# The attention stage of a graph network on one core: SyncE issues all transfers of a group at one moment, behind the transposes of the node rows

## The reference, cut to what matters

```python
h = (x @ gat_W).reshape(n, H, C1)
a_src = jnp.einsum('nhc,hc->nh', h, att_src)
a_dst = jnp.einsum('nhc,hc->nh', h, att_dst)
logits = jax.nn.leaky_relu(a_src[src] + a_dst[dst], negative_slope=0.2)
alpha = _segment_softmax(logits, dst, n)
msg = h[src] * alpha[:, :, None]
x1 = jax.ops.segment_sum(msg, dst, num_segments=n).reshape(n, H * C1) + gat_bias
x1 = _prelu(x1, prelu1_a)
q = x1 @ Wq + bq
k = x1 @ Wk + bk
v = x1 @ Wv + bv
```

## Time and profile before

| what | us |
|---|---|
| median of 3 runs | 6158.78 |
| lowest and highest | 6152.38, 6185.52 |
| the profiled execution, its own time | 6170.1 |
| its span, first to last instruction | 6168.3 |
| busy PE, DVE, ACT, POOL | 3904.2, 2719.5, 718.2, 3232.2 |

### The profile page before, as it was taken

The page is one execution under the profiler, slowest core; times in us unless marked ns, Lnnn a source line. Parts: engine busy times, 40 slices in busy tenths (PEclk is TensorE's granted clock), DMA queues, the critical chain, the costliest instruction groups (busy, mean ns, idle before and its releaser), DMA issues. The chain is left out here.

```text
span 6168.3 us, 73822 instructions
## 1 busy us (share of the span) xinstructions
PE 3904.2 (63%) x14562; PEld 2847.0 (46%) x14563; DVE 2719.5 (44%) x9904; ACT 718.2 (12%) x2361; POOL 3232.2 (52%) x3351
## 2 busy tenths in 40 slices
PE   3555555563556655554667666767674777777777
PEld 2343434342444444443455555555552555555555
DVE  5443434342333233332444444444453555555555
ACT  3000000000000000000111111101110212222122
POOL 5466666644555555554444444444433555555553
PEclk8677777776777777776777776777786888888889
DMA  7344444433333333332333333333322444343432
GB/s 182 80 107 106 107 105 107 106 86 88 106 107 106 106 107 107 107 101 87 89 94 97 93 97 93 96 95 95 96 78 84 113 119 122 111 119 112 118 115 84
DMA packets 334355, 636.43 MB, mean 103 GB/s; under 512 B 86166, under 2 KB 213124, under 8 KB 333828
## 3 DMA queue, kind: packets, MB, share of 16 engines
q0 software_dynamic: 159744, 441.43, 27.5%
q1 hardware_dynamic: 170437, 185.56, 9.6%
q10 hardware_dynamic: 3648, 3.67, 0.2%
HBM read 565.59 MB, written 64.79 MB: 102 GB/s over the span
## 5 line engine op out<-in xcount | busy, mean ns | idle before, releaser
L1211 POOL DMA_INDIRECT G<-t,srcI x828 | 807.6, 975 | 914.2 <-DVE g_Gp L1425 676.3
L1841 POOL DMA_INDIRECT G<-t,srcI x824 | 785.7, 953 | 629.6 <-PE g_ps L2208 371.7
L228 POOL DMA_INDIRECT G<-t,srcI x832 | 820.7, 986 | 516.1 <-issue 238.7
L859 POOL DMA_INDIRECT G<-t,srcI x828 | 793.6, 958 | 536.7 <-ACTq L1133 298.8
L2198 PE MATMUL g_psA<-g_win,g_ohT 128*128 128x257 f32 x1664 | 614.1, 456 | 374.7 <-DVE g_L L1943 177.6
L737 PE MATMUL g_ps<-G,g_oh 128*128 128x257 f32 x1664 | 555.6, 500 | 142.8 <-DVE g_oh L587 142.8
L1554 PE MATMUL g_psA<-g_win,g_ohT 128*128 128x4 f32 x1664 | 345.1, 328 | 439.1 <-issue 416.4
L1943 DVE CUSTOM_DVE_ANT_0 g_junk<-G,g_psA 128x257 f32<-128x257 f32 x832 | 348.5, 419 | 557.9 <-DMA G<-t,srcI 239.2
L1554 PEld LDWEIGHTS g_psA<-g_win,g_ohT 128*128 128x128 f32 x1664 | 359.6, 316 | 459.6 <-issue 459.1
L2208 PE MATMUL g_ps<-G,g_oh 128*128 128x257 f32 x1664 | 558.2, 422 | 0.0
L2198 PEld LDWEIGHTS g_psA<-g_win,g_ohT 128*128 128x128 f32 x1664 | 321.7, 217 | 511.2 <-DVE g_L L1943 222.6
(11 more groups left out here) (372 smaller groups left out, 4825.9 us busy)
## 6 DMA issues: line engine op xcount, KB each, us to landing
G<-t,srcI POOLq DMA_INDIRECT x3328
g_relb<-relrow SPq DMA_DIRECT2D x104, 512.0 KB
t<-g_t SPq DMA_DIRECT2D x53, 132.0 KB, 1.7
g_rec<-t SPq DMA_DIRECT2D x53, 132.0 KB
g_own<-t SPq DMA_DIRECT2D x53, 129.5 KB
x<-g_o SPq DMA_DIRECT2D x53, 128.5 KB
g_rec<-x SPq DMA_DIRECT2D x53, 128.5 KB
t<-g_t4r SPq DMA_DIRECT2D x53, 128.5 KB, 2.0
```

Source lines behind the costliest of these rows:

```text
L228: pool.indirect_dma_start(G[:, b, u, 0:width], None, m.t1, IOA(ap=m.srcI[:, g * UW + u:g * UW + u + 1], axis=0)).then_inc(s_g[b][u // QW], 16)
L859: pool.indirect_dma_start(G[:, b, u, :], None, table, IOA(ap=m.srcI[:, g * UW + u:g * UW + u + 1], axis=0)).then_inc(s_g[b][u // QW], 16)
L1211: pool.indirect_dma_start(G[:, b, u, :], None, m.t3, IOA(ap=m.srcI[:, g * UW + u:g * UW + u + 1], axis=0)).then_inc(s_g[b], 16)
L1841: pool.indirect_dma_start(G[:, b, u, :], None, m.t4, IOA(ap=m.srcI[:, g * UW + u:g * UW + u + 1], axis=0)).then_inc(s_g[b][u // QW], 16)
```

## The change

SP's order within a body is changed. The other engines' code is the same, and so are the transfers, their sizes and what each waits for; `turn` loses its last call, and `store_rows` comes first in it.

```diff
             def turn(n, start, before):
+                store_rows(n, before)
                 sp.wait_ge(s_used, n + 1)
                 hold(m, sp)
                 load(start)
-                store_rows(n, before)
-                store(n, before)
...
                 logits, agg, lead = parts(k)
+                if logits:
+                    d0, = load_wide(nc, m, sp, k, ("d0",))
+                    nwin, xb = load_pack(nc, m, sp, k)
+                    with sp.If(nwin > 1):
...
+                if agg:
+                    d0, last = load_wide(nc, m, sp, k - 1, ("d0", "last"))
+                    nwin, xb = load_pack(nc, m, sp, k - 1)
+                    base = xb + (k - 1)
+                    turn(base, d0, last)
                 if lead:
                     if agg:
                         sp.wait_ge(s_s2, k)
...
                     sp.wait_ge(s_pa, k + 1)
                     hold(m, sp)
                     window(k + 2, b % 2)
-                if logits:
-                    d0, = load_wide(nc, m, sp, k, ("d0",))
-                    nwin, xb = load_pack(nc, m, sp, k)
-                    with sp.If(nwin > 1):
...
-                if not isinstance(k, int) or k + 2 < NGW:
                     sp.wait_ge(s_s1, k + 1)
                     hold(m, sp)
                     places(k + 2, b)
                 if agg:
-                    d0, last = load_wide(nc, m, sp, k - 1, ("d0", "last"))
-                    nwin, xb = load_pack(nc, m, sp, k - 1)
-                    base = xb + (k - 1)
-                    turn(base, d0, last)
+                    store(base, last)
```

More of the change, by code:

```diff
@@ L1255, in body @@
                 logits, agg, lead = parts(k)
+                if logits:
+                    d0, = load_wide(nc, m, sp, k, ("d0",))
+                    nwin, xb = load_pack(nc, m, sp, k)
+                    with sp.If(nwin > 1):
+                        with sp.Fori(1, nwin) as i:
+                            sp.wait_ge(s_xpa, xb + i)
+                            hold(m, sp)
+                            sp.dma_start(winx[:], m.t3[bass.ds(window_start(nc, d0, i), P), ROW:AGW]).then_inc(s_xwin, 16)
+                if agg:
[3 more added lines that the diff above has]
+                    turn(base, d0, last)
                 if lead:
@@ L1284, in body @@
                             turn(base + i, window_start(nc, d0, i), window_start(nc, d0, i - 1))
+                            store(base + i, window_start(nc, d0, i - 1))
             sp.sem_inc(s_xpa, 1)
```

## The result

| what | us |
|---|---|
| kernel after, median of 20 runs | 6195.18 (6173.07 to 6208.41) |
| kernel before, median of 20 runs on the same chip | 6168.45 (6152.38 to 6185.52) |
| ratio, 95% interval | 1.0042 (1.0035 to 1.0049) |
| the profiled execution of after, its own time and span | 6191.96, 6190.2 |

The change costs 26 us, 0.42%. That is under the 0.5% that the forecast took for "same", and yet the interval leaves no doubt that it is slower; the +4 us of the forecast are too small by a factor of more than six.

A forecast was written before the change was run, and what follows sets the result against it. A loop of POOL and DVE was taken to bound the kernel, 34.3 us a group. 48 x 0 for the groups, 1.3 us for relb and 2.7 us for rec gave +4.0 us on 6158.8, so 6163, range 6150 to 6185.

The forecast's parts named there:

- rival B: Slower: DVE's wait for relb outruns its room, set in from a 5.0 us delay; 6241 or 6265 us; chance 0.12.
- the release: Moment in each batch when the slow stretch ends and DVE gets past L1314; forecast unchanged, 23.1 us after the first gather.
- The period: Time of one attention group: POOL's 14.3 us wait for the weighing plus 20.05 us issuing its batch, 34.3 us.
- Store, masks, window: SP's t4 store stays put, row masks and window move out of the batch or behind the store: 0 each.
- Places, the wait: relb issued 3.3 us after the store, landing 4.0 us later; DVE waits 1.7 us at L1320 (0 to 7.2).
- Places, what hides it: DVE's 1.7 us wait goes into 5.0 us of room before the release: 0 for each of 48 groups.
- rival A: Faster: less SP work in the batch lets DVE do three comparisons before the release; 91 us, 6068; chance 0.20.
- Record, in the groups: Load of own rows rec, moved behind the store, lands 1.7 us before L1348 wants it: 0 per group.
- Record, at the end: At the attention stage's end rec, issued 0.7 us behind the last store, lands 2.0 us later: 2.7 us on the path.
- The end as a whole: After the last batch: 1.3 us for loads of relb without cover plus 2.7 us for rec, +4.0 us.
- Rival C: Slower: relb's bytes stretch the batch of gathers, 2.1 us in each of 48 groups, 100 us, 6259; chance 0.06.
- Rival D: SP isn't there in time, so its transfers don't go out at one moment; waits stay idle, 6159; chance 0.04.

The follow-up runs named there:

- e1: The kernel after, with the load of the places relb issued early again, ahead of the store: ratio 1.0024 to the kernel before.
- e7: The kernel before, with only the load of the record rec moved behind the t4 store: ratio 1.0016 to the kernel before.
- e6: The kernel after, with only the load of the record rec put ahead of the t4 store again: ratio 1.0006 to the kernel before.
- e3: The kernel before, with one more 512 KB load in each batch into a buffer nobody reads: ratio 1.0008 to the kernel before.
- e2: The kernel before, with only the load of the places relb moved behind the t4 store: ratio 1.0001 to the kernel before.
- e8: The kernel before, with POOL's wait split so each four gathers wait for their own weighed quarter: ratio 0.9941 to the kernel before.
- e11: The kernel before, with DVE's comparisons L1314 a turn later and POOL's wait split in quarters: ratio 0.9933 to the kernel before.
- e12: The kernel before, with comparisons a turn later and ahead of the row scans, and POOL's wait in quarters: ratio 0.9736, 5936.66 us against 6093.96.

## Why the prediction was right or wrong

The call "same, within 0.5%" held, but by luck: the forecast had nothing in the groups, and the runs have a cost there that happens to be small. The median of 6195.18 us lies outside the forecast's own 6150 to 6185 and inside the reach of up to 6220 that was left for rival B. The difference of the two kernels is 22 us off the forecast (the kernel before, with 20 runs, is another 10 us above the 6158.8 that the forecast started from). Of the signs named beforehand, POOL's wait went from 14.3 to 14.8 us, within the 0.7, the release stayed, and L1320 has its new wait; but the wait ahead of L1477 grew where it was to shrink.

- *The period*: right. 20.05 us of batch, the release, then DVE's list. The release is at 23.1 us in both kernels, as predicted.
- *Store, masks, window*: about right. e1 against e7 leaves them 0.08%, inside both intervals. The lag from the store to the places is 3.5 us in the median, 3.3 forecast.
- *Places, the wait*: right in kind, 1.7 us forecast, 2.6 us measured. From the issue of the load (1.3 us after the first gather in the median, forecast 0.9) to L1321 (6.0 us) it is 4.7 us, not 4.0.
- *Places, what hides it*: this is the step that failed. "So 1.7 us goes into that room: 0 for each of the 48 groups." The room of 5.0 us was that of one transpose in one group, and the delay was carried into it one to one. The median delay of 2.7 us at L1321 became 7.1 us at the scans, and the latest scans start at 22.25 us, where the latest of before start at 13.05. And the room isn't free: "idle time for DVE with much to spare" holds comparisons, and each that no longer fits costs 0.6 us. I had seen that price from the gain side (rival A, 1.90 us for three) and not asked what a delay does to the one or two comparisons that ran in the batch already. In place of 48 x 0 the runs show 46 x 0.41 = 18.6 us.
- *Record, in the groups*: 0 forecast, the other half of the failed "48 x 0". e7 shows about 7 us in its trace, and the record put ahead again in after (e6) returns 24 us, the end of the stage included. DVE hardly waits for it (5.8 us in after). What passes the delay on I could not settle; PE's products of the node rows stand 0.7 us later in the batch there (in the median), and whether that is cause or result isn't told apart.
- *Record, at the end*: 2.7 us forecast, 4.2 us for this step in after, 4.0 in e7 (8.76 - 4.74).
- *The end as a whole*: +4.0 forecast, +5.8 measured.
- *Rival A*: no sign of it. *Rival C*: refuted by e3. *Rival D*: SP was in time. *Rival B*: true in its first half: the delay is multiplied in the batch. The price it named, DVE waiting behind the release for what comes late, is seen in five groups of after, 4 us; the rest of the 19 us is comparisons that slid behind the release, a cost that no rival had. It doesn't set in at a point either, but in steps of 0.6 us, from a delay below 5.0 us.
- The Trainium skill's advice in "DMA: Bandwidth & Descriptors", section "Rules for kernel authors", to issue early and wait late, was cited against the change and then given no weight. This case agrees with its direction: the lead of the places was cut from 14.7 us to about 2 us, L1321 waits 2.6 us a group, and e1, which gives the lead back, is 0.16% to 0.18% faster than after, by intervals that touch.

## What to carry to other kernels

Slack in front of a stall isn't one number: list what the stalled engine gets done before the stall ends, in every group and not in one, since each piece that slides behind it is paid in full. Where an engine's instructions crawl, a delay ahead of the crawl is to be multiplied and not subtracted (here 2.7 us became 7). Work whose inputs are a turn old belongs ahead of the first wait for something fresh: moving four comparisons there was worth more (2.0%, with the batch already earlier) than any order of the transfers.

## What the runs showed of the hardware

- DVE and PE keep their pace for a while into a batch of back-to-back gathers, and then crawl. DVE's first wait after about 5 us of a batch is long: scans whose PE transposes started 4.0 to 4.5 us after the first gather began at 5.9 us in the median (21 groups of before), those of 5.0 to 5.5 us at 11.0 us (8 groups). On PE the same eight products took 0.62 us at 9.2 us into the batch and 8.5 us at 11.1 us (3533.38 to 3541.90).
- PE carries part of its work past the release: about 4 of the 32 scores were done before it in before, 0.5 in after, and what is left runs behind it at 0.22 us a score (5.49 us for 25). The last of PE's products of the node rows starts 1.0 us later in after (2.2 us after the next first gather, 1.2 in before, both in the median), and the next transposes L1627 start 0.8 us later (5.4 and 4.7). That one late group makes the next one late isn't shown: from one group to the next the starts of the scans correlate by 0.45 in before, by 0.01 in after.
- A load of 512 KB, issued about 2.7 us into the batch (e3), changed neither the release (22.8 us as in e2) nor the period (33.99, e2 34.04); the bytes moved by SP don't explain the crawl. What does, no run here tells.
- The release stands at nearly the same time after the first gather whichever instruction DVE has reached by then: in the median at 22.8 to 23.1 us for the comparisons in before, after and e1 to e7, at 23.0 us for the scans in e8 and at 22.8 us for the scans in e11 and e12. With POOL's wait in quarters the batch begins 3.4 us earlier in DVE's list; the release moves along with the batch, and L1500 starts 27.6 us after the first gather, not 24.9, since 2.2 us of scans and what follows them and 2.4 us of comparisons now stand behind it.
